# The first layer of the top-1 experts computed transposed, its weights loaded tile by tile

## What is computed

```
top_idx = argmax(x @ gate_w.T + gate_b + expert_bias)      # one of 8 experts per token
h   = relu(x @ w1[e] + b1[e])                              # 256 -> 1024
y   = h @ w2[e] + b2[e]                                    # 1024 -> 256
out = x_residual + y
```

## Time and profile before

| | |
|---|---|
| three runs | 958.2, 960.7, 963.5 us; median 960.7 |
| profiled execution, span from first to last instruction | 958.8 us |
| TensorE matmul busy | 799.9 us, 83% |
| VectorE, ScalarE, GpSimd busy | 503.9, 315.6, 421.5 us |
| granted TensorE clock, mean | 0.913 |
| bytes moved by DMA | 87.30 MB, 91 GB/s |

### The profile page before, as it was taken

How to read it: one execution, slowest core, us unless ns; L and a number is a source line. 1 busy time by engine, 2 the same in 40 slices (tenths; PEclk the granted TensorE clock), 3 DMA queues, 4 the chain that set the end, 5 groups by cost and what they waited for, 6 DMA issues and landing times. The chain is left out here.

```text
span 958.8 us, 15942 instructions
## 1 busy us (share of the span) xinstructions
PE 799.9 (83%) x4041; PEld 595.9 (62%) x4043; DVE 503.9 (53%) x1598; ACT 315.6 (33%) x896; POOL 421.5 (44%) x463
## 2 busy tenths in 40 slices
PE   4799999585699599999994789988693299999995
PEld 3688888343366366777762567777572167777773
DVE  2788886542133565555543799999552123333331
ACT  1355554011122144444431344444330033333331
POOL 1243442033767354554543776667442233333321
PEclk8899999598899799999998799999785599999998
DMA  7333233402020144444453235545896211111000
GB/s 193 139 114 112 88 122 105 117 13 16 13 22 0 36 132 134 140 138 140 136 126 97 72 108 170 179 174 126 108 126 134 65 34 38 48 33 45 25 23 2
DMA packets 57926, 87.30 MB, mean 91 GB/s; under 512 B 22073, under 2 KB 43033, under 8 KB 56476
## 3 DMA queue, kind: packets, MB, share of 16 engines
q1 hardware_dynamic: 43996, 57.35, 23.3%
q0 software_dynamic: 13600, 27.33, 11.0%
q10 hardware_dynamic: 288, 2.10, 0.6%
HBM read 67.04 MB, written 22.44 MB: 93 GB/s over the span
## 5 line engine op out<-in xcount | busy, mean ns | idle before, releaser
L590 POOL DMA_INDIRECT U<-normed,idx x95 | 91.1, 959 | 98.1 <-issue 64.8
L575 POOL TENSOR_TENSOR U<-U,mx 128x1232 f32<-128x1232 f32 x32 | 72.2, 2256 | 100.9 <-DVE mx L1207 100.6
L1039 PE MATMUL bank<-R,U 128*128 x380 | 103.7, 396 | 5.9 <-issue 3.9
L757 ACT ACTIVATE X<-bank,U 128x128 f32<-128x128 f32 x184 | 50.1, 383 | 127.3 <-PE bank L1076 127.3
L1092 PE MATMUL bank<-R,X 128*128 x184 | 84.2, 601 | 0.0
L1103 PE MATMUL bank<-R,X 128*128 x368 | 83.3, 379 | 1.0 <-ACT X L757 1.0
L1103 PEld LDWEIGHTS bank<-R,X 128*128 128x128 f32 x368 | 69.8, 190 | 20.1 <-issue 11.7
L1039 PEld LDWEIGHTS bank<-R,U 128*128 128x128 f32 x380 | 65.4, 192 | 19.3 <-issue 11.7
L568 POOL DMA_INDIRECT U<-expert_out,slot_cur x64 | 64.3, 1005 | 22.4 <-issue 15.2
L507 POOL DMA_INDIRECT table<-tok_cur,slot_cur x64 | 61.6, 962 | 26.5 <-issue 22.0
L623 POOL DMA_INDIRECT out<-U,idx_out x23 | 23.4, 1019 | 106.9 <-DVE idx L1118 67.2
(11 more groups left out here) (187 smaller groups left out, 1681.4 us busy)
## 6 DMA issues: line engine op xcount, KB each, us to landing
R<-in_w SPq DMA_DIRECT2D x16, 1024.0 KB
R<-in_gu SPq DMA_DIRECT2D x8, 1024.0 KB, 5.5
expert_out<-U SPq DMA_DIRECT2D x48, 128.0 KB
expert_out<-xr SPq DMA_DIRECT2D x47, 128.0 KB
normed<-xr SPq DMA_DIRECT2D x32, 128.0 KB
R<-in_down SPq DMA_DIRECT2D x8, 512.0 KB, 3.7
x<-X SPq DMA_DIRECT2D x16, 128.0 KB
X<-in_x ACTq DMA_DIRECT2D x1, 1536.0 KB, 8.7
```

What stands on the lines that cost most here:

```text
L575: pool.tensor_tensor(s3, s3, mx[u][:, :].unsqueeze(2).to_broadcast([P, H, S2]), ALU.subtract).then_inc(T["sub"], 1)
L590: pool.indirect_dma_start(xg0[u], None, xn_d[0], bass.IndirectOffsetOnAxis(idx[u][:, :], 0)).then_inc(EX[0]["gath"][u], 16)
L757: ins = act.activation(hT1[:, c, :], bank[5 + g][:, (c % 4) * P:(c % 4 + 1) * P], ACT.Relu, bias=b1_of[u][:, c:c + 1])
L1039: mm = pe.matmul(bank[2 + u][:, 0:2 * F0], xgT0[u][:, c, :], gu_w[:, c, bass.ds(e, 1), :].rearrange("p a n -> p (a n)"), start=(c == 0), s ...
```

## The change

The weights of the first layer become the stationary operand and the tile's rows the streamed one, so the result comes out with the hidden index on the partitions, as the second layer needs it. Sixteen matmuls of 128 columns take the place of four of 512, and the eight transposes and the two copies go. ScalarE makes relu of the first half of the hidden blocks, VectorE that of the second half, straight from PSUM. `hT1` and the second layer's bank become double. The whole resident `w1` goes: SyncE loads the 1 MB of the tile's expert into one of two buffers for every tile, after the first layer two tiles before is done, and the eight loads of `w1` during attention go.

```diff
+        w1_of, o = [], 0
+        for i in range(2):
+            v, o = cut(R1, o, (KC, F1))
+            w1_of.append(v)
...
-                sp.dma_start(w1_w[:, :, bass.ds(e, 1), :], A["w1"][:, :, bass.ds(e, 1), :]).then_inc(w1_in, 16)
...
             phase_barrier(sp, 5)
+            def first_weights(i):
+                if on(i, 0, TILES1):
+                    e = load_expert(sp, sp_experts, i, par(0, 4), E1)
+                    need(sp, EX[1]["h_mm"], 2 * (i - 1))
+                    sp.dma_start(w1_of[par(0)], A["w1"][:, :, bass.ds(e, 1), :].rearrange(
+                        "p c a f -> p c (a f)")).then_inc(w1_in[par(0)], 16)
+            steps(sp, first_weights, 0, 4, PLAN1 - 4, TILES1 - 1, 4)
...
 # ScalarE
-                if on(s, 0, TILES1):
-                    for g in range(2):
-                        act.wait_ge(X1["ht_mm"], 2 * s + g + 1)
...
                 if on(s, 2, TILES1):
                     act.wait_ge(X1["xt_mm"], s + 3)
+                    need(act, X1["h_mm"], 2 * s + 2)
...
+                if on(s, 1, TILES1):
+                    act.wait_ge(X1["b1"], s + 2)
+                    act.wait_ge(X1["h_mm"], 2 * s + 3)
+                    need(act, X1["dn_mm"], s)
+                    for c in range(FC1 // 2):
+                        ins = act.activation(hT1[v][:, c, :], bank[1 + 2 * v][:, c * P:(c + 1) * P], ACT.Relu,
+                                             bias=b1_of[v][:, c:c + 1])
+                    ins.then_inc(X1["h"], 1)
 # TensorE
-            pe.wait_ge(w1_in, 16 * E1)
...
-                    for g in range(2):
-                        pe.wait_ge(X1["h"], 2 * s + g + 1)
-                        need(pe, X1["ht"], 2 * s + g - 1)
-                        for c in range(4 * g, 4 * g + 4):
-                            mm = pe.transpose(bank[5 + g][:, (c % 4) * P:(c % 4 + 1) * P],
-                                              h1[u][:, c * P:(c + 1) * P], ident[:, :])
...
                     pe.wait_ge(X1["xt"], s + 2)
-                    need(pe, X1["h"], 2 * s)
-                    for a in range(2):
+                    pe.wait_ge(w1_in[par(1)], landed(s + 1, 2))
+                    need(pe, X1["h"], s)
+                    need(pe, X1["ht"], s)
+                    for f in range(FC1):
                         for c in range(KC):
-                            mm = pe.matmul(bank[1 + 2 * v + a][:, :], xgT1[v][:, c, :],
-                                           w1_w[:, c, bass.ds(e, 1), a * 512:(a + 1) * 512].rearrange(
-                                               "p a n -> p (a n)"),
+                            mm = pe.matmul(bank[1 + 2 * v + f // 4][:, (f % 4) * P:(f % 4 + 1) * P],
+                                           w1_of[v][:, c, f * P:(f + 1) * P], xgT1[v][:, c, :],
                                            start=(c == 0), stop=(c == KC - 1))
...
-                        if c % 4 == 0:
-                            pe.wait_ge(X1["ht"], 2 * s + c // 4 + 1)
-                        mm = pe.matmul(bank[7][:, 0:D], hT1[:, c, :],
+                        if c == 0:
+                            pe.wait_ge(X1["h"], s + 1)
+                        if c == FC1 // 2:
+                            pe.wait_ge(X1["ht"], s + 1)
+                        mm = pe.matmul(bank[6 + u][:, 0:D], hT1[u][:, c, :],
 # VectorE
-                    for a in range(2):
-                        dve.wait_ge(X1["h_mm"], 2 * s + a + 3)
-                        dve.tensor_copy(h1[v][:, a * 512:(a + 1) * 512], bank[1 + 2 * v + a][:, :]).then_inc(X1["h"], 1)
+                    wait_apart(dve, X1["b1"], s + 2)
+                    dve.wait_ge(X1["h_mm"], 2 * s + 4)
+                    need(dve, X1["dn_mm"], s)
+                    for c in range(FC1 // 2, FC1):
+                        ins = dve.tensor_scalar(hT1[v][:, c, :], bank[2 + 2 * v][:, (c % 4) * P:(c % 4 + 1) * P],
+                                                b1_of[v][:, c:c + 1], 0.0, ALU.add, ALU.max)
+                    ins.then_inc(X1["ht"], 1)
```

More of the change, by code:

```diff
@@ L110, in build @@
         gu_w, _ = cut(R1, 0, (KC, E0, 2 * F0))
-        w1_w, _ = cut(R1, 0, (KC, E1, F1))
+        w1_of, o = [], 0
+        for i in range(2):
+            v, o = cut(R1, o, (KC, F1))
+            w1_of.append(v)
         down_w, o = cut(R2, 0, (E0, D))
@@ L180, in build @@
         o = 0
-        xg1, xgT1, h1 = [], [], []
+        xg1, xgT1, hT1 = [], [], []
         for i in range(2):
-            for lst, shape in ((xg1, (D,)), (xgT1, (KC, P)), (h1, (F1,))):
+            for lst, shape in ((xg1, (D,)), (xgT1, (KC, P)), (hT1, (FC1, P))):
                 v, o = cut(X, o, shape)
                 lst.append(v)
-        hT1, o = cut(X, o, (FC1, P))
         assert o <= NT * D
@@ L285, in build @@
         experts0_in = sem("experts0_in")
-        w1_in = sem("w1_in")
+        w1_in = [sem("w1_in0"), sem("w1_in1")]
         w2_in = sem("w2_in")
@@ L490, in _ @@
             phase_barrier(sp, 5)
+            sp_experts = [sp.alloc_register(f"sp_expert{i}") for i in range(4)]
+            def first_weights(i):
[5 more added lines that the diff above has]
+            steps(sp, first_weights, 0, 4, PLAN1 - 4, TILES1 - 1, 4)
             phase_barrier(sp, 6)
@@ L749, in experts1 @@
                 u = par(0)
-                if on(s, 0, TILES1):
-                    for g in range(2):
-                        act.wait_ge(X1["ht_mm"], 2 * s + g + 1)
-                        if g == 0:
-                            need(act, X1["dn_mm"], s)
-                            act.wait_ge(X1["b1"], s + 1)
-                        for c in range(4 * g, 4 * g + 4):
-                            ins = act.activation(hT1[:, c, :], bank[5 + g][:, (c % 4) * P:(c % 4 + 1) * P], ACT.Relu,
-                                                 bias=b1_of[u][:, c:c + 1])
-                        ins.then_inc(X1["ht"], 1)
+                v = 1 - u
                 if on(s, 2, TILES1):
                     act.wait_ge(X1["xt_mm"], s + 3)
+                    need(act, X1["h_mm"], 2 * s + 2)
                     act.activation(xgT1[u].rearrange("p c n -> p (c n)"), bank[0][:, 0:D],
                                    ACT.Copy).then_inc(X1["xt"], 1)
+                if on(s, 1, TILES1):
[6 more added lines that the diff above has]
+                    ins.then_inc(X1["h"], 1)
             experts1_steps(act, experts1)
@@ L1069, in experts1 @@
                 v = 1 - u
-                if on(s, 0, TILES1):
-                    for g in range(2):
-                        pe.wait_ge(X1["h"], 2 * s + g + 1)
-                        need(pe, X1["ht"], 2 * s + g - 1)
-                        for c in range(4 * g, 4 * g + 4):
-                            mm = pe.transpose(bank[5 + g][:, (c % 4) * P:(c % 4 + 1) * P],
-                                              h1[u][:, c * P:(c + 1) * P], ident[:, :])
-                        mm.then_inc(X1["ht_mm"], 1)
                 if on(s, 2, TILES1):
@@ L1523, in experts1 @@
                     e = load_expert(dve, dve_experts, s + 1, par(1, 4), E1)
-                    need(dve, X1["ht"], 2 * (s - 1) + 2)
+                    need(dve, X1["h"], s)
+                    need(dve, X1["ht"], s)
                     dve.tensor_copy(b1_of[v], b1T[:, bass.ds(e, 1), :].rearrange("p a n -> p (a n)")).then_inc(
                         X1["b1"], 1)
-                    for a in range(2):
-                        dve.wait_ge(X1["h_mm"], 2 * s + a + 3)
-                        dve.tensor_copy(h1[v][:, a * 512:(a + 1) * 512], bank[1 + 2 * v + a][:, :]).then_inc(X1["h"], 1)
+                    wait_apart(dve, X1["b1"], s + 2)
[5 more added lines that the diff above has]
+                    ins.then_inc(X1["ht"], 1)
                 if on(s, 0, TILES1):
@@ L1533, in experts1 @@
                     need(dve, X1["out"][par(2, 4)], landed(s - 2, 4))
-                    dve.tensor_tensor(y1[u], bank[7][:, 0:D], b2_b[:, bass.ds(e, 1), :].rearrange("p a n -> p (a n)"),
+                    dve.tensor_tensor(y1[u], bank[6 + u][:, 0:D], b2_b[:, bass.ds(e, 1), :].rearrange("p a n -> p (a n)"),
                                       ALU.add).then_inc(X1["y"], 1)
```

8 lines of the change are left out of this document (4 added, 4 removed).

## The result

| | before | after |
|---|---|---|
| median of the runs, us | 961.8 | 950.6 (946.8 to 955.0) |
| ratio | | 0.9875, 95% interval 0.9838 to 0.9913 |
| profiled execution, us (span) | 960.7 (958.8) | 949.2 (947.2) |
| TensorE busy, us | 799.9 | 776.4 |
| mean granted clock | 0.913 | 0.909 |

The forecast was 936, range 923 to 949. Faster is right; the size is wrong by 15 us. Two repeats of the changed kernel beside the kernel before gave 0.9879 [0.9834, 0.9924] and 0.9897 [0.984, 0.9955].

The account below looks back on a forecast made before the run. TensorE's own instruction time was taken to bound the last stage, several engines and transfers alternating in attention. Span 958.8 - 18.3 (last stage) - 6 (attention) = 934.5 us, 936 as a median; range 923 to 949.

Parts of the forecast that it names:

- Transposes removed, first layer, step 7.23: Last stage: eight transposes fewer per tile, -20.0 us; reshaped first layer, +2.7 us; a step of 7.23 us.
- Stalls at the ends, -2.0: Last stage: TensorE's waits at the first transposes and around the last tile's relu go, -2.0 us.
- Relu and copies at nothing: Last stage: ScalarE's and VectorE's relu work hides behind the second layer of the tile before, costing nothing.
- The stream at nothing: Last stage: loading 1 MB of w1 a step costs nothing, with 5 us in hand.
- stream becomes the bound: Rival, last stage: w1 loads set the pace, steps of 8.1 to 10.3 us, up to 1003 us; chance 0.06.
- loads don't hide: Rival, last stage: stationary-operand loads add to the streaming, +80 us, 1016 us in all; chance 0.02.
- First load, +1.0 (0 to 3): Head of the last stage: only the first w1 load is exposed after barrier 5, costing 1.0 us.
- Attention without the w1 loads, -6 (0 to -18): Attention of layer 1: without w1 loads the long gather wait and GpSimd's drain shorten by 3 us each.
- the tail doesn't move: Rival, end of attention: dropping the w1 loads gains nothing there, 942 us; chance 0.22.
- The clock rival: Rival, attention's end: an earlier tail keeps TensorE's clock full, some 6 us more, besides 12 rather than 6: 924; chance 0.13.

Follow-up runs that it names:

- w2 early: Changed kernel with the eight w2 loads issued after each of attention's first eight tiles, none beside the one-word scatters; ratio 0.9768, median 943.5 us.
- the scatters behind: Changed kernel with GpSimd's first two one-word scatters issued behind the last tiles' gathers instead of ahead; ratio 0.9866, attention 241.3 us.

## Why the prediction was right or wrong

- **Transposes removed, first layer, step 7.23.** Right: 7.25. A first layer of 32 records takes 3.57 (3.56 forecast), 0.112 us a record. By the Trainium skill (TensorE: Matmul & The Clock Gate, "The mechanism") weight loads overlap matmuls in flight only where the row groups differ; this run disagrees: the sum of load and stream would be 7.2 us. The same section also lets a load into a background weight buffer past, and no run here tells whether that is what happened.
- **Stalls at the ends, -2.0.** Right in kind: 929.96 + 6.92 has no gap. With the terms above it makes -19.3 against -18.6 measured. The start isn't free, though: the first first layer takes 4.83 to 6.16 us, partly at half clock, where it took 4.94 before.
- **Relu and copies at nothing.** Right: they lie beside TensorE's work and are done before it asks.
- **The stream at nothing.** Right, shown by taking it away. DMA share 0.50 as forecast. The rivals "stream becomes the bound" and "loads don't hide" are out.
- **First load, +1.0 (0 to 3).** Too small: +3.8. I priced the weights' own landing (6.7 us behind barrier 5, near the 5.8 forecast) and gave the gathers "perhaps 763". The second tile's rows landed at 768.6 instead: four gathers share the DMA engines with 2 MB. They had the engines to themselves before.
- **Attention without the w1 loads, -6 (0 to -18).** This is the step that failed. I read a share of 0.78 at 83 GB/s as a queue that gets shorter if half of its bytes go. It isn't one: the high share is what the scatters do to the load beside them (0.87 at 67 GB/s with them, 0.89 at 254 without), and without w1 attention took 3 to 6 us more. The step that I had wrong is this reading; why the missing loads cost time, and don't just bring none, stays open. Even the rival "the tail doesn't move" (942) was too kind. The bounds should have taken in a loss: I had no row that excluded one.
- **The clock rival** (an earlier tail at full clock, 6 us) had a mechanism that exists: 6.5 us, in one profile of the kernel before and in w2 early. None of the three profiles of the kernel after shows it.
- **Small slips, without effect.** By the terms' own bounds the stage lies between -12 and -22, not -13 and -21. The last w1 load leaves SyncE's queue at 726.0, not at 733.
- The Trainium skill's rule on transfers under 512 bytes (DMA: Bandwidth & Descriptors, "Specifications") would have put the term of attention at 0 and was the better guide. The runs without scatters agree with its direction, 33 to 38 us for 16 transfers of words; it doesn't say how a load elsewhere can help.

The sum with the measured terms: 958.8 - 18.6 + 3.8 + 5.7 = 949.7 of span; the profile had 947.2, having come to attention 2.8 earlier.

## What to carry to other kernels

A high DMA share at a low rate wasn't traffic that could be thinned out here: look for word-sized transfers beside it, and move the large loads away from them (about 10 us, in either version). When a load moves to the head of a stage, price what the first gathers lose to it, not only its own landing. And take more than one profile before a term of 5 us is read from a stretch that waits for DMA: this one spreads over 11, and more than half of that is the granted clock of two steps. Compare the clock of the same steps first.

## What the hardware showed that I had not expected

- Gathers behind a 128-word scatter in GpSimd's queue started late where a large load ran beside it: those issued 148.5 us into attention had their first packet at 156.3 in the kernel after, 7.8 us behind the issue. With w2 early (issued 148.3) it came at 150.0, though the last still ended at 161.4; with the scatters behind (issued 145.5) at 147.3, and the last ended at 153.6.
- A wait for a DMA can outlast its last packet by 5 us while the DMA engines stand idle (share 0.00), and the increments of other DMAs that write to HBM come late with it.
- The same step of attention took 12.5 us at a granted clock of 0.50 and 7.2 at 1.00, and one kernel without an edit showed both.
- The first 32 matmul records of the stage took 4.83, 5.06 and 6.16 us in three profiles of one kernel, where all later ones take 3.57.
